# A pre-LN decoder layer with a Mamba2 mixer on one core: single-tile steps on every engine, and decays from broadcast rows instead of difference matmuls

## What is computed

```python
h = rmsnorm(layernorm(x)) * norm_w
proj = h @ in_proj_w.T                # 8192 gate, 8192 hid, 1024 B, 1024 C, 128 dt
hBC = silu(causal_conv(hBC, conv_w, conv_b))      # four taps
dt = softplus(dt + dt_bias);  A = -exp(A_log)
A_cs = cumsum(A * dt)                 # in chunks of 128 tokens, 128 heads
L = exp(segsum(A * dt))               # exp(A_cs[i] - A_cs[j]) for i >= j, else 0
y = ((C @ B.T) * L) @ (hid * dt) + Dp * hid       # per head of 64 columns
yg = y * silu(gate)
y = yg * rsqrt(mean of yg*yg over the group's 1024 columns + EPS) * gnorm_w
x = x + y @ out_proj_w.T
```

## Time and profile before

| what | before |
|---|---|
| runs | 919.88, 920.33, 919.98 us |
| median | 919.98 us |
| span of the profiled execution | 918.4 us |
| the median less that span | 1.58 us |
| TensorE busy | 860.0 us, 94%, 4666 matmuls |
| TensorE's weight loads | 649.8 us, 71% |
| VectorE busy | 682.9 us, 74% |
| ScalarE busy | 540.8 us, 59% |
| GpSimd busy | 469.7 us, 51% |
| moved by DMAs | 61.56 MB, mean 67 GB/s |
| granted TensorE clock, loop | full |

### The profile page before, as it was taken

One profiled execution on the slowest core, in us unless ns is written; L12 is line 12 of the kernel. 1 busy time (PEld: TensorE's weight loads), 2 busy tenths in 40 slices (PEclk: granted clock), 3 DMA queues, 4 the chain that ended last, 5 costly groups with the idle time before them and its releaser, 6 DMA issues.

```text
span 918.4 us, 15226 instructions
## 1 busy us (share of the span) xinstructions
PE 860.0 (94%) x4666; PEld 649.8 (71%) x4666; DVE 682.9 (74%) x939; ACT 540.8 (59%) x1004; POOL 469.7 (51%) x366
## 2 busy tenths in 40 slices
PE   4888899999999999999999999999999999888478
PEld 3676577777778777877777777877787777656255
DVE  7796799559982989379965998299937996597753
ACT  3533688348853777357834885377735783566343
POOL 6335267536665458345753566535834575555020
PEclk9999799999999999999999999999999999889779
DMA  5223012211223122221222121212222222401001
GB/s 145 76 76 92 24 48 94 81 59 56 84 63 91 50 65 74 79 63 51 93 68 71 47 90 61 90 46 70 73 80 58 56 92 64 146 24 35 0 1 46
DMA packets 34656, 61.56 MB, mean 67 GB/s; under 512 B 4740, under 2 KB 5252, under 8 KB 34628
## 3 DMA queue, kind: packets, MB, share of 16 engines
q1 hardware_dynamic: 34628, 61.21, 22.1%
HBM read 59.75 MB, written 1.44 MB: 67 GB/s over the span
## 4 chain that ended last, share of the span: by engine, by line
issue 40%; PE 26%; POOL 21%; DVE 7%; ACT 3%; POOLq 1%; DMA 1%; SPq 0%; DVEq 0%; ACTq 0%
POOL w_lo L464 12%; POOL sqsum L486 5%; PE ps_in L1141 4%; PE ps_in L1143 4%; PE ps_in L1142 4%; PE ps_o L1141 3%; PE ps_o L1143 2%; PE ps_o L1142 2%; POOL wo_lo L470 2%; POOL eB L479 2%; PE ps_t L1200 1%; PE ps_t L1207 1%; PE ps_y L1270 1%; PE ps_df L1239 1%; PE ps_in L1423 1%
## 5 line engine op out<-in xcount | busy, mean ns | idle before, releaser
L1141 PE MATMUL ps_in<-h_hi,w_hi 128*128 128x512 f32 x544 | 226.1, 416 | 5.3 <-DVE hid L869 2.1
L464 POOL TENSOR_TENSOR w_lo<-raw,w_hi 128x512 fp32r<-128x512 f32 x144 | 187.2, 1322 | 71.9 <-ACT w_hi L563 71.6
L1142 PE MATMUL ps_in<-h_lo,w_hi 128*128 128x512 f32 x544 | 214.3, 394 | 0.0
L1143 PE MATMUL ps_in<-h_hi,w_lo 128*128 128x512 f32 x544 | 214.1, 394 | 0.0
L479 POOL TENSOR_TENSOR eB<-eB,gmB 128x512 f32<-128x512 f32 x64 | 98.1, 1532 | 207.0 <-ACT eB L610 207.0
L869 DVE SCALAR_TENSOR_TENSOR hid<-ps_in,curc,hid 128x510 f32<-128x510 f32 x180 | 134.4, 746 | 18.1 <-ACT hid L583 13.1
L602 ACT ACTIVATE ps_df<-ps_df 128x256 f32<-128x256 f32 x185 | 74.2, 430 | 119.2 <-PE ps_df L1239 118.3
L1141 PEld LDWEIGHTS ps_in<-h_hi,w_hi 128*128 128x128 f32 x544 | 102.8, 189 | 42.0 <-issue 17.9
L470 POOL TENSOR_TENSOR wo_lo<-rawo,wo_hi 128x512 fp32r<-128x512 f32 x64 | 83.4, 1309 | 75.8 <-ACT wo_hi L568 75.1
L1143 PEld LDWEIGHTS ps_in<-h_hi,w_lo 128*128 128x128 f32 x544 | 103.0, 189 | 22.8
L1142 PEld LDWEIGHTS ps_in<-h_lo,w_hi 128*128 128x128 f32 x544 | 103.2, 190 | 17.9
(11 more groups left out here) (257 smaller groups left out, 1524.4 us busy)
## 6 DMA issues: line engine op xcount, KB each, us to landing
raw<-in_w_in SPq DMA_DIRECT2D x144, 256.0 KB, 2.8
rawo<-in_w_out SPq DMA_DIRECT2D x64, 256.0 KB, 2.7
res<-in_x SPq DMA_DIRECT2D x4, 256.0 KB, 3.6
out_x<-res SPq DMA_DIRECT2D x4, 256.0 KB, 2.2
raw<-in_ctx SPq DMA_DIRECT2D x3, 256.0 KB, 3.4
mov<-acs_parts SPq DMA_DIRECT2D x32, 12.0 KB
sta<-acs_parts SPq DMA_DIRECT2D x32, 12.0 KB
th<-in_ctx SPq DMA_DIRECT2D x2, 256.0 KB, 4.2
```

The lines of the kernel that those rows point to most:

```text
L464: pool.tensor_tensor(w_lo[:, i % W_RING, :], raw[:, i % RAW_RING, :], w_hi[:, i % W_RING, :].bitcast(F32), ALU.subtract).then_inc(s_lo, 1)
L1141: pe.matmul(dst, lh, rh, start=first, stop=False)
L1142: pe.matmul(dst, lh, rl, start=False, stop=False)
L1143: return pe.matmul(dst, ll, rh, start=False, stop=last)
```

## The change

Every engine now runs `step(n, t)`: one tile of each kind per step, all stages of the mixer at fixed lags behind the projection of tile (n, t). In a step TensorE projects the hid tile t, turns the hid tile t-1, makes the outputs of tile t-2, multiplies z tile t-3 into the output projection, and projects the gate tile t; `lagged` finds group and tile of such an index, across the border of a group too. B and C of the next group are projected in steps 3 and 5, the scores of a group in its step 0, the token sums of the group before at the head of step 2. `ps_o` holds the output projection of a group in four banks of its own.

The difference matmuls, `mov`, `sta` and the clamps are gone. The running sums go to DRAM as fp32 rows, in the form that one step needs (two heads, three blocks, two sequences of 128); `load_rows` copies them to all 128 partitions of `e`, a ring of four (2 heads x 3 blocks x 256 x 4 bytes x 128 partitions = 0.79 MB a step). GpSimd's `mask_rows` writes -1e30 over the upper halves of the two diagonal blocks with two AFFINE_SELECTs, ScalarE takes eight exponentials a step with the negated running sum as its bias, four of 128 x 256 and four of 128 x 128, GpSimd multiplies the middle block (`decays_off`) and VectorE the two others (`decays_diagonal`) with the scores.

The context is quantised by GpSimd in group 0, three operations a step; before, ScalarE did part of it in the last group. The dt product comes first, in front of B and C, and the dt chain must be done by steps 1 and 2 of group 0. The one-hot matrices of the permutation are made by GpSimd in front of the last `group_rms`. Weight loads have a ring of six instead of three.

The diff, cut to its core (`...` marks what is left out):

```diff
-            def diffs(m, t, banks):
-                if t == 0:
-                    pe.wait_ge(s_rows, 16 * 8 * (m + 1))
-                for k in banks:
-                    if isinstance(m, int) and m == last_m and t:
-                        pe.wait_ge(s_exp, 3 * CT * m + (3 if t == 1 else 3 * (t - 1) + k + 1))
-                    else:
-                        wait(pe, s_exp, since(3 * CT * m, 3 * t + k, 2))
-                    bank = df_bank(m, t, k)
-                    heads = (k,) if k < 2 else (0, 1)
-                    for hh in heads:
-                        h = 2 * t + hh
-                        q = slice(32 * (h // 4), 32 * (h // 4) + 6)
-                        for b in range(BATCH):
-                            at = b * SEQ if k < 2 else b * SEQ + P
-                            width = SEQ if k < 2 else P
-                            to = b * SEQ if k < 2 else (hh * BATCH + b) * P
-                            last = pe.matmul(bank[:, to:to + width], sta[q, h % 4, at:at + P],
-                                             mov[q, h % 4, at:at + width], start=True, stop=True)
-                    last.then_inc(s_df, 1)
...
-            def exps(m, t, banks):
-                for k in banks:
-                    act.wait_ge(s_df, 3 * CT * m + 3 * t + k + 1)
-                    blocks = diagonal(df_bank(m, t, k), k)
-                    act.activation(blocks, blocks, ACT.Relu).then_inc(s_cl, 1)
-                for k in banks:
-                    act.wait_ge(s_cl, 3 * CT * m + 3 * t + k + 1)
-                    if k == 0:
-                        if isinstance(m, int) and m == 0 and t == 0:
-                            act.wait_ge(s_res, TT)
-                        wait(act, s_y, since(CT * m, t, 2))
-                    dst = eA[:, t % 2, k, :] if k < 2 else eB[:, t % 2, :, :].rearrange("p a n -> p (a n)")
-                    act.activation(dst, df_bank(m, t, k), ACT.Exp, scale=-1.0).then_inc(s_exp, 1)
+            def exps(m, q):
+                u = CT * m + q
+                act.wait_ge(s_msk, u + 1)
+                if q == 0:
+                    act.wait_ge(s_curg, 2 * m + 2)
+                for late in (0, 1):
+                    for hh in range(2):
+                        for b in range(BATCH):
+                            h = 2 * q + hh
+                            a = e[:, q % E_RING, hh, 2, b, :] if late else e[:, q % E_RING, hh, 0:2, b, :]
+                            last = act.activation(a, a, ACT.Exp, bias=nag[:, 2 * b + late, h:h + 1])
+                    last.then_inc(s_exp, 1)
...
-            def rows(g):
-                for q in range(4):
-                    src = acs_dram[:, bass.ds(g * GH + 4 * q, 4), :]
-                    sp.dma_start(mov[32 * q:32 * q + 3, :, :], src).then_inc(s_rows, 16)
-                    sp.dma_start(sta[32 * q + 3:32 * q + 6, :, :], src).then_inc(s_rows, 16)
+            def load_rows(m, q):
+                u = CT * m + q
+                wait(sp, s_y, u - E_RING + 1)
+                row = acs_dram[bass.ds(2 * u, 2), :, :, :].rearrange("h k b i -> (h k b i)")
+                sp.dma_start(e[:, q % E_RING, :, :, :, :].rearrange("p h k b i -> p (h k b i)"),
+                             row.partition_broadcast(P)).then_inc(s_rows[q % E_RING], 16)
...
+            def rows_arrived(m, q):
+                pool.wait_ge(s_rows[q % E_RING], 16 * (CT // E_RING * m + q // E_RING + 1))
+            def mask_rows(m, q):
+                for k in (0, 2):
+                    d = e[:, q % E_RING, :, k, :, :]
+                    last = pool.affine_select(out=d, in_=d, compare_op=ALU.is_ge, fill=MASKED, base=0,
+                                              pattern=[[0, 2], [0, BATCH], [1, P]], channel_multiplier=-1)
+                last.then_inc(s_msk, 1)
+            def decays_off(m, q):
+                u = CT * m + q
+                pool.wait_ge(s_exp, 2 * u + 1)
+                if q == 0:
+                    pool.wait_ge(s_gm, 2 * m + 2)
+                o = e[:, q % E_RING, :, 1, :, :].rearrange("p h b i -> p h (b i)")
+                pool.tensor_tensor(o, o, gm[:, 1, :, :].rearrange("p b i -> p (b i)").unsqueeze(1)
+                                   .broadcast_to([P, 2, BATCH * P]), ALU.mult).then_inc(s_mb, 1)
...
+            def context(c):
+                pool.wait_ge(s_ctx[c % 2], 16 * (c // 2 + 1))
+                if c == 0:
+                    pool.wait_ge(s_qd, 1)
+                a = craw[:, c % 2, :]
+                pool.tensor_scalar(a, a, qd[:, 1:2], qs[:, 3:4], ALU.mult, ALU.add).then_inc(s_cs, 1)
+                pool.wait_ge(s_cs, c + 1)
+                pool.tensor_scalar(a, a, 0.0, 255.0, ALU.max, ALU.min).then_inc(s_cc, 1)
+                pool.wait_ge(s_cc, c + 1)
+                pool.tensor_scalar(q2[:, c, :], a, MAGIC, -(MAGIC + 128.0), ALU.add, ALU.add).then_inc(s_q2, 1)
...
+            def step(n, t):
+                if t == 2 and not is_first(n):
+                    group_rms(n - 1)
+                ahead = (n, t + 1) if t + 1 < CT else (n + 1, 0)
+                tiles = [] if is_last(n) and t + 1 == CT else step_tiles(*ahead)
+                lead = is_first(n) and t < 3
+                if tiles:
+                    split_in(ahead[0], tiles[0])
+                m, q = lagged(n, t, 2)
+                if tiles:
+                    split_in(ahead[0], tiles[1])
+                if is_first(n) and t == 2:
+                    rows_arrived(0, 0)
+                    mask_rows(0, 0)
+                    rows_arrived(0, 1)
+                    mask_rows(0, 1)
+                    decays_off(0, 0)
+                if not (is_first(n) and t < 2):
+                    decays_off(*lagged(n, t, 1))
+                    rows_arrived(n, t)
+                    split_out(m, q)
+                    mask_rows(n, t)
+                if len(tiles) > 2:
+                    split_in(ahead[0], tiles[2])
+                if q and not lead:
+                    add_square(m, q)
+                if is_first(n):
+                    if t == 0:
+                        for k in range(TT):
+                            start_residual(k)
+                    context(t)
...
-            def iteration(n, do_in, do_ssd):
-                m = n - 1
-                lag = 1 if do_ssd else 2
-                if do_in and not (isinstance(n, int) and n == 1):
-                    project(n, 0, do_ssd)
-                    if not do_ssd:
-                        dt_product()
-                    project(n, 1, do_ssd)
-                for t in range(CT):
-                    if do_ssd:
-                        outputs(m, t)
-                        if t + 1 < CT:
-                            diffs(m, t + 1, (0, 1))
-                    if do_in:
-                        project(n, 2 + 2 * t, do_ssd)
-                    if do_ssd and t + 1 < CT:
-                        diffs(m, t + 1, (2,))
-                    if do_in:
-                        project(n, 3 + 2 * t, do_ssd)
-                        if not do_ssd and t == 2:
-                            dt_turn()
-                        if t >= lag:
-                            turn(n, t - lag)
-                if do_ssd:
-                    out_pair(m, 0, (0, 1), do_in)
-                    out_pair(m, 1, (0, 1), do_in)
-                if not do_ssd:
-                    turn(n, CT - 2)
-                    project(n + 1, 0, True)
+            def step(n, t):
+                tiles = step_tiles(n, t)
+                lead = is_first(n) and t < 3
+                if t == 2 and not is_first(n):
+                    token_sums(n - 1)
+                project(n, tiles[0])
+                if is_first(n) and t == 1:
+                    dt_turn()
+                if is_first(n) and t == 2:
+                    scores(0)
+                    turn(0, 0)
+                if not lead:
+                    turn(*lagged(n, t, 1))
+                    outputs(*lagged(n, t, 2))
+                    out_tile(*lagged(n, t, 3))
+                if t == 0 and not lead:
+                    scores(n)
+                for tile in tiles[1:]:
+                    project(n, tile)
+                if is_first(n) and t == 2:
+                    turn(0, 1)
+                    outputs(0, 0)
...
+            for k in range(DK):
+                pool.tensor_scalar(take[:, k, :], perm_row[:, :], dcol[:, k:k + 1], None, ALU.is_equal)\
+                    .then_inc(s_tp, 1)
+                pool.tensor_scalar(put[:, k, :], iota_row[:, :], perm_col[:, k:k + 1], None, ALU.is_equal)\
+                    .then_inc(s_tp, 1)
+            group_rms(last_m)
```

1254 lines of the change are left out of this document (607 added, 647 removed).

## The result

| | before | changed kernel |
|---|---|---|
| median | 920.15 us | 943.27 us |
| ratio, 95% interval | | 1.0244 [1.0228, 1.0261], slower |
| span of the profiled execution | 918.4 us | 939.3 us |
| TensorE busy | 860.0, 4666 matmuls | 821.1, 4158 matmuls |
| VectorE, ScalarE, GpSimd busy | 682.9, 540.8, 469.7 | 696.5, 542.9, 624.8 |

The forecast was 884 us, 850 to 910, faster with 0.90. The kernel got 2.4% slower: the sign is wrong. The work went as forecast, 39 us of TensorE's busy time and all of L1239; what wasn't forecast stands beside it: time in which TensorE waits, and time in which it runs at the lower clock. One of the changed kernel's four runs took 1167.91 us at a granted clock of 0.648; the ratio goes by the other three.

A forecast was written before the change was run, and what follows sets the result against it. TensorE's queue was taken as the bound: 735.0 us of its work, plus 18 ramp, 28.7 token-sum waits and 11 clock, made 792.7; plus 21.5 and 68.2 for the end, 882.4 of span, so 884 us, range 850 to 910.

The forecast's parts named there:

- The step: TensorE's loop: one step's hid projection, turn, outputs, output projection tile and gate projection take 10.34 us.
- the matmuls removed being worth their place: TensorE's loop: removed matmuls save their whole place in its queue, 8.9 us a group, were nobody late.
- eight exponentials: ScalarE, each step: eight short exponentials with a pointer bias, taken at 2.8 us.
- the masks: GpSimd, two each step: 512 elements, one input, not in the trace, taken at 0.6 us each.
- the wait for the last square: Token sums, head of step 2: TensorE stands still 4.1 us once a group, seven times, 28.7 us.
- The three queues are covered in an ordinary step: VectorE, ScalarE and GpSimd in the loop: their edits cost nothing, with 2 to 3 us of cover.
- the one collision above: Ahead of the token sums: decays_diagonal and split_out, both reading two SBUF operands, do not overlap; 0.8 us added.
- port bound, 7%: Rival, 7%: VectorE's four two-input operations a step each wait for GpSimd; from 0.6 us each the step passes 11.
- I take 1.2 us for each of seven waits and 3 for the ramp: Granted clock: TensorE's lower level behind the token sums' waits and in the ramp costs 11 us, bounds 0 and 20.
- The waits of the ramp: Start, group 0: TensorE waits of 3.5, 0.6, 6.5, 4 and 3 us, together 18, bounds 10 and 26.
- the one-hots: End, GpSimd: eight one-hot tiles ahead of group_rms, at 0.55 to 1.30 us each; 0.56 each puts first add_output at 21.5.
- The 8% for slower: Whole kernel: chance given to a slower result, against 0.90 for faster by more and 0.02 for within.

The follow-up runs named there:

- e7: Changed kernel with the edits of e1 and e2, and the eight one-hot tiles made between the second and third rstd power: 868.63 us, ratio 0.9429.
- e1: Changed kernel with GpSimd adding a group's eighth square ahead of split_out and the masks of its step 1: 897.01 us, ratio 0.9749.
- e2: Changed kernel with VectorE taking gated of step 5 ahead of decays_diagonal instead of behind it: 915.22 us, ratio 0.9959.
- e8: e7 with each mask cut to 128 x 16 elements and Tanh in place of Exp: 865.67 us, ratio 0.9412.
- e4: Changed kernel with 18 more matmuls, results never read, in TensorE's wait for the last square, in seven groups: 925.08 us, ratio 1.0062.

## Why the prediction was wrong

Of 939.3 - 882.4 = 56.9 us of span, by stretch. The forecast's parts follow from its sum: the first token sums would start at 152.0, six periods of 96.1, 80.1 to the last sums, 5.5 to the first add_output, 68.2 to the end.

| stretch | forecast | measured | more |
|---|---|---|---|
| to the first token sums | 152.0 | 168.1 | 16.1 |
| six groups | 576.6 | 606.3 | 29.7 |
| from the seventh to the last sums | 80.1 | 84.3 | 4.2 |
| to the first add_output | 5.5 | 13.3 | 7.8 |
| to the end | 68.2 | 67.3 | -0.9 |

**What held.** The step (10.28 for 10.34), the matmuls removed being worth their place (e7: 91.0 a group, forecast 90.8 with nobody late), eight exponentials in 2.87 us (2.8), the masks at 0.61 (0.6), the wait for the last square and what stands ahead of it (3.9 for 4.1), shown by e1. No wait of TensorE in the loop ends with a DMA: the rows landed in 4.4 us and the engines were 0.39 busy.

**Step that failed first: "The three queues are covered in an ordinary step: I cost their edits at nothing there, and the cover is those 2 to 3 us".** I laid out a step without a B or C tile. In steps 3 and 5 TensorE has a third projection, whose weights GpSimd splits a step earlier; that puts the next hid tile on the bank of the gate tile only one projection behind it. The port conflict that I counted once a group ("the sum takes only the one collision above") stretches four VectorE operations by 3.7 us in step 5: 1.98 us of wait, 0.9 of clock on average, 4.3 a group in all by e2. The rival named for this (port bound, 7%) had the pair of engines right and the mechanism wrong: not four small waits in every step, but one late operation on a bank that TensorE needs.

**Second: "I take 1.2 us for each of seven waits and 3 for the ramp: 11; the bounds are 0 and 20".** The price came from one row, outputs behind a wait of 1.18 us. Measured are 2.8 on average behind the sums' wait of 3.9 and 0.9 behind the gate's, 3.75 a group. In the ramp the granted clock is 0.86 in the first 50 us, for 0.97 before, and 0.93 for 0.95 up to 150. The waits of the ramp from the dt product to the sums are 23.9 us (forecast 18) and the sums' own 5.0 (4.1); the start is late by 16.1. What is left, 9 us beyond the 3 that I gave, is the clock by this reckoning: 48 projection matmuls stand 0.43 us apart instead of 0.23 there, some 10 us, but no run took the clock out of the ramp. Together the clock costs some 36 us (22.5 in six groups, 1.6 behind the seventh sums, 12 in the ramp) where I had 11: the largest term of the error, with the gate's wait (12 us in six groups) and the one-hots.

**Third: the one-hots "at 0.56 each".** They take 1.56, outside the 0.55 to 1.30 that I gave; I had bounded a comparison with an operand per partition by an iota below and a two-input operation above. 8 us at the end. The context's clip and rounding on GpSimd are in the same class: 1.95 us each, in group 0.

**The 8% for slower** were for a mechanism of every step. The forecast had each cost apart, took each at a middle value with all others in place, and gave no case in which a second wait in each group, slow matmuls behind both waits and a slow ramp come together; that case is what came.

## What to carry to other kernels

When a full engine's queue gets shorter, lay out each kind of step against the other engines, above all the uneven ones (an extra tile, a bank that comes round sooner), since the shortened queue arrives earlier at every hand-over. On each engine, put what the full one waits for ahead of what nobody waits for: here moving one addition and one gate operation in their queues was worth 60 us in six groups (e7), where easing GpSimd's load by 66 us (e8) was worth 3. Price a wait of TensorE with the slow matmuls behind it, and over several groups, since one place shows either all of them or none, and check an idle engine's price for an operation before moving it there.

## What the runs showed of the hardware

- Behind one and the same wait of 1.94 to 2.00 us TensorE went on at the lower clock in 18 of 24 groups (the projection took 4.05 to 4.45 us) and at full clock in 6 (2.84 to 2.87); behind 1.1 us it did so in none of six, behind 3.7 to 5.0 us in all seven of the changed kernel. Filling the longer wait with matmuls of no use (e4) gave back 18 us of 943.
- GpSimd's operations on 128 x 512 fp32 elements differ by three: 0.61 for a mask, 0.76 for a scale and offset, 1.28 for a subtraction of two tensors, 1.56 for a comparison with a value per partition, 1.95 for a clip. VectorE makes the comparison in 0.47, and in 1.5 beside GpSimd.
- Four VectorE operations that take 3.3 us alone took 7.1 beside two-input operations of GpSimd, and no semaphore's wait shows it.
